# Attention stage of a graph transformer step: x and weights loaded in parts, projections by token halves, a column of ones beside the values, key and query sketches placed between projections

## What is computed

```
xn = layernorm(x)
q, k, v = xn @ Wq, xn @ Wk, xn @ Wv            # 8 heads of 64
phi(z)  = (0.125 * (z @ G1) * (z @ G2)) ** 2   # per head; G1, G2 are 64 x 64
kv      = phi(k).T @ v                          # per head 64 x 64
den     = phi(q) @ sum(phi(k), over tokens)
attn    = (phi(q) @ kv) / (den + 1e-6)
x       = x + biases + attn @ Wp
m       = relu(xn) + 1e-7                       # first message of the graph part
A[dst, src] += 1                                # adjacency of 20625 edges, sorted by dst
...                                             # 3 graph convolutions, then the experts
```

## Time and profile before

| what | value |
|---|---|
| median of 3 runs | 1040.75 us (1038.95 to 1041.92) |
| the profiled execution | 1040.16 us, of which the span of the core is 1038.3 us |
| mean granted TensorE clock in it | 0.954 |
| PE busy | 940.6 us (91%) |
| DVE busy | 709.4 us (68%) |
| ACT busy | 447.8 us (43%) |
| POOL busy | 392.2 us (38%) |
| first one-hot row of the adjacency | 156.7 us after the start |

### The profile page before, as it was taken

The page is one execution under the profiler, slowest core; times in us unless marked ns, Lnnn a source line. Parts: engine busy times, 40 slices in busy tenths (PEclk is TensorE's granted clock), DMA queues, the critical chain, the costliest instruction groups (busy, mean ns, idle before and its releaser), DMA issues. The chain is left out here.

```text
span 1038.3 us, 13178 instructions
## 1 busy us (share of the span) xinstructions
PE 940.6 (91%) x4324; PEld 696.8 (67%) x4324; DVE 709.4 (68%) x1325; ACT 447.8 (43%) x694; POOL 392.2 (38%) x322
## 2 busy tenths in 40 slices
PE   2979598996999999998999989889999999999980
PEld 2879585443888778886788868666666666666650
DVE  4463548988665467678767786758777776766675
ACT  3442510013344353543444522466666666666640
POOL 4500000000750035410751115366666666666640
PEclk9985898998999999999999998989999999999995
DMA  6200003312420022201220052559999999999868
GB/s 173 83 1 1 1 1 118 121 57 88 133 72 23 1 80 92 83 1 51 87 86 17 20 186 87 187 196 328 338 339 334 355 333 324 380 348 345 312 161 209
DMA packets 57100, 159.73 MB, mean 154 GB/s; under 512 B 13840, under 2 KB 21590, under 8 KB 48595
## 3 DMA queue, kind: packets, MB, share of 16 engines
q1 hardware_dynamic: 44755, 147.63, 41.7%
q0 software_dynamic: 12288, 11.36, 3.8%
HBM read 152.71 MB, written 25.58 MB: 172 GB/s over the span
## 5 line engine op out<-in xcount | busy, mean ns | idle before, releaser
L260 PE MATMUL ps<-split_operands 128*125 128x512 f32 (+5 forms) x690 | 272.9, 396 | 31.4 <-DVE split_operands L986 5.7
L261 PE MATMUL ps<-split_operands 128*125 128x512 f32 (+5 forms) x690 | 266.1, 386 | 0.0
L262 PE MATMUL ps<-split_operands 128*125 128x512 f32 (+5 forms) x690 | 265.4, 385 | 0.0
L630 POOL DMA_INDIRECT yrow_scratch<-work,row_i x64 | 150.9, 2358 | 97.3 <-ACT work L891 94.8
L260 PEld LDWEIGHTS ps<-split_operands 128*125 128x125 f32 (+3 forms) x690 | 135.0, 196 | 61.3 <-issue 13.6
L376 POOL TENSOR_TENSOR split_operands<-work,split_operands 128x512 fp32r<-128x512 f32 x66 | 83.6, 1296 | 202.1 <-ACT split_operands L358 189.9
L262 PEld LDWEIGHTS ps<-split_operands 128*125 128x125 f32 (+3 forms) x690 | 135.2, 196 | 26.7
L261 PEld LDWEIGHTS ps<-split_operands 128*125 128x125 f32 (+3 forms) x690 | 135.6, 196 | 24.0
L1366 DVE TENSOR_TENSOR gate_up_lo<-expert_weights,split_operands 128x2048 fp32r<-128x2048 f32 x64 | 146.3, 2286 | 3.8 <-ACT split_operands L873 3.6
L873 ACT ACTIVATE split_operands<-expert_weights 128x2048 fp32r<-128x2048 f32 x64 | 121.9, 1905 | 3.2 <-DMA expert_weights<-experts_in 3.1
L1834 PE MATMUL ps<-expert_weights,work 128*117 128x512 f32 x256 | 120.3, 592 | 0.5 <-issue 0.5
(11 more groups left out here) (214 smaller groups left out, 1286.3 us busy)
## 6 DMA issues: line engine op xcount, KB each, us to landing
expert_weights<-experts_in SPq DMA_DIRECT2D x64, 1024.0 KB
expert_weights<-experts_in SPq DMA_DIRECT2D x64, 512.0 KB
work<-w_in SPq DMA_DIRECT2D x12, 1024.0 KB, 5.2
yrow_scratch<-work SPq DMA_DIRECT2D x5, 1500.0 KB
split_operands<-yrow_scratch SPq DMA_DIRECT2D x4, 1120.0 KB
work<-wmix_in SPq DMA_DIRECT2D x4, 1024.0 KB, 7.6
work<-cw_in SPq DMA_DIRECT2D x3, 1024.0 KB, 5.2
work<-rows_in SPq DMA_DIRECT2D x10, 256.0 KB, 4.7
```

The costliest lines, as they stand in the source:

```text
L260: pe.matmul(o, a[1], b[0], start=start, stop=False)
L261: pe.matmul(o, a[0], b[1], start=False, stop=False)
L262: return pe.matmul(o, a[0], b[0], start=False, stop=stop)
L630: pool.indirect_dma_start(yrow, bass.IndirectOffsetOnAxis(ap=row_i[:, e:e + 1], axis=0), OS[e % 4], None, bounds_check=last_row, oob_is_er ...
```

## The change

- The plan holds Wv and Wk as two halves each. SP loads the first two tiles of x, the halves of Wv, then the other three tiles, the bias rows and the halves of Wk; ACT issues the last 13 rows of x. DVE does statistics and norms of two tiles first and of the others one at a time, between the work on the values. The transposes of tiles 2 to 4 stand inside the products of the values.
- The projections take a half of the tokens through all four chunks, then the other half.
- The low part of the values moves from POOL to DVE. The bias rows that POOL adds to x are summed first (6 additions in place of 10), and this is done after the query sketches.
- The value tiles are 130 columns a chunk, with a column of ones on either side (written by POOL). The key-value product is 15 instead of 25 matmuls a chunk, of 256 columns each that hold 128 values and the ones; the separate product with ones is gone. The evacuation of it takes 65 columns a head and chunk instead of 128.
- Key sketches start after six key projections and stand between the others; query sketches stand between the last query projections; the messages are done beside the first key projections.
- Membership is a comparison per tile boundary (4 operations instead of 10, 2 matmuls instead of 5), and the ranges are worked out in the third round of the attention output. The buffers of this preparation have places of their own, so that the index tables are made at the start.
- PE starts the adjacency without waiting for the last addition to x, and the zeros that clear the scratch in memory are ready from the start, so SP starts that clearing (5 transfers of 1500 KB) behind the attention weights instead of at the start of the adjacency.

```diff
-        VV = pair(o_e, NT, D, p=T)
-        KT = pair(o_e + 5120, KD, TP)
+        VV = pair(o_e, NT, KD * 130, p=T)
+        KT = pair(o_e + 5200, KD, TP)
...
-            return two_banks(4 if t % 2 else 6)
-
-        kv_bank = ps[:, 0:2, :].rearrange("p b (c n) -> p (b c) n", c=2)
+            b = 6 if t % 2 else 4
+            return ps[0:T, b:b + 2, :].rearrange("p b (c n) -> p (b c) n", c=2)
+
+        def values(v, t):
+
+            return v[:, t, :].rearrange("p (c n) -> p c n", c=KD)[:, :, 1:129]
+
+        def kv_window(c):
+
+            return cut(130 * c if c % 2 == 0 else 130 * (c + 1) - 256, 256)
+
+        def kv_out(c):
+
+            return ps[:, c // 2, cut(256 if c % 2 == 0 else 0, 256)]
+
+        def kv_part(h):
+
+            return ps[64 * h:64 * h + 64, 0:2, 126:386].rearrange("p b (a n) -> p b a n", a=2)[:, :, :, cut(65 * h, 65)]
...
-        piece("wv", wmv[2], WMA)
-        piece("wk", wmv[1], WMB)
+        for n, m, w in (("wv", 2, WMA), ("wk", 1, WMB)):
+            for k in range(2):
+                piece(f"{n}{k}", wmv[m][:, 2 * k:2 * k + 2, :], sub(w, A_, cut(2 * k, 2), A_))
...
-            by_rows(XO, x.rearrange("(t p) f -> p t f", p=T), "x_in", (sp, sp))
+            xv = x.rearrange("(t p) f -> p t f", p=T)
+            sp.dma_start(XO[0:112, 0:2, :], xv[0:112, 0:2, :]).then_inc(S("x_in"), 16)
...
-            for n in ("wv", "wk"):
-                load(n)
+            load("wv0")
+            load("wv1")
+            sp.dma_start(XO[0:112, 2:NT, :], xv[0:112, 2:NT, :]).then_inc(S("rw_in"), 16)
...
+            load("wk0")
+            load("wk1")
...
-            sp.wait_ge(S("vector_consts"), 2)
+            sp.wait_ge(S("vector_consts"), 1)
...
+            for t in range(NT):
+                for part in range(2):
+                    last = pool.memset(f(VV[part][:, t, :]).rearrange("p (c n) -> p c n", c=KD)[:, :, 0:130:129], 1.0 - part)
+            last.then_inc(S("pool_consts"), 1)
...
+            pool.wait_ge(S("pk_lo"), PKU + 8)
+            g1(pool.tensor_tensor(BC2, BC2, BC1[:, D:H], ALU.add))
             for t in range(NT):
-                g1(pool.tensor_tensor(XO[:, t, :], XO[:, t, :], BC1[:, D:H], ALU.add))
                 pool.tensor_tensor(XO[:, t, :], XO[:, t, :], BC2, ALU.add).then_inc(S("x_rows"), 1)
...
-                pool.wait_ge(S("v_hi"), t + 1)
-                pool.tensor_tensor(VV[1][:, t, :], MT[t % 2][0:T, :], f(VV[0][:, t, :]), ALU.subtract).then_inc(S("v_lo"), 1)
...
+            for u in range(3, 6):
+                proj(u)
+            act.wait_ge(S("v_lo"), NT)
+            pk_scale(0)
+            proj(6)
+            pk_square(0)
+            pk_scale(1)
+            proj(7)
+            pk_square(1)
+            proj_sb(8)
+            pk_scale(2)
+            pk_scale(3)
+            pk_square(2)
+            pk_scale(4)
+            pk_square(3)
+            proj_sb(9)
+            pk_square(4)
+            proj_hi(8)
+            proj_hi(9)
+            split_hi("wp")
+            proj(10)
+            proj(11)
...
+            proj(12)
+            proj(13)
             pq_scale(0)
-            for u in range(8):
-                if u + 1 < 8:
-                    pq_scale(u + 1)
-                pq_square(u)
+            proj(14)
+            pq_scale(1)
+            pq_square(0)
+            pq_scale(2)
+            pq_square(1)
+            proj(15)
+            for u in range(3, 8):
+                pq_scale(u)
+                pq_square(u - 1)
...
+            row_norm(0)
+            row_norm(1)
+            tr_lo(0)
+            split_lo("wv0", dve)
+            split_lo("wv1", dve)
+            tr_lo(1)
+            dve.wait_ge(S("rw_in"), 32)
+            row_var(2)
+            row_var(3)
+            row_norm(2)
+            dve.wait_ge(S("first_rows_in"), 64)
+            v_sum(0)
+            tr_lo(2)
+            row_norm(3)
+            row_var(4)
+            v_sum(1)
+            v_low(0)
+            tr_lo(3)
+            row_norm(4)
+            split_lo("wk0", dve)
...
+            for u in range(4):
+                message(0, u)
+                proj_lo(u)
+            message(0, 4)
+            proj_lo(4)
+            split_lo("wq", dve)
+            proj_lo(5)
+            pk_mul(0)
+            proj_lo(6)
+            pk_low(0)
+            pk_mul(1)
+            proj_lo(7)
...
+            proj_lo(12)
+            proj_lo(13)
+            pq_mul(0)
...
-            dve.memset(zero_b, 0.0).then_inc(S("vector_consts"), 1)
...
+                near = iota_odd[:, j // 2, :] if j % 2 else iota_h[:, cut(T * j, T + 1)]
...
-                        dve.tensor_scalar(one_hot_dst[:, i, :], iota_h[:, 0:T + 1], dstrel[:, j, bass.ds(lo + q * G + i, 1)], None,
+                        dve.tensor_scalar(one_hot_dst[:, i, :], near, dstf[:, bass.ds(lo + q * G + i, 1)], None,
...
-            for u in range(8, 16):
-                if u == 10:
-
-                    pe.wait_ge(S("pk_lo"), NT)
-                    pe.wait_ge(S("v_lo"), NT)
-                    pe.wait_ge(S("vector_consts"), 1)
-                    for c in range(KD):
-                        b, o = c // 2, 256 * (c % 2)
-                        for t in range(NT):
-                            mm3(ps[:, b, cut(o, P)], sub(PK, A_, t, cut(c * P, P)), sub(VV, A_, t, cut(c * P, P)), t == 0, t == NT - 1)
-                        for t in range(NT):
-                            for part in range(2):
-                                last = pe.matmul(ps[:, b, cut(o + P, P)], PK[part][:, t, cut(c * P, P)], ones_r[:],
-                                                 start=(t == 0 and part == 0), stop=(t == NT - 1 and part == 1))
...
+            def key_values():
+                pe.wait_ge(S("pk_lo"), NT)
+                pe.wait_ge(S("v_lo"), NT)
+                pe.wait_ge(S("pool_consts"), 3)
+                for c in range(KD):
+                    for t in range(NT):
+                        last = mm3(kv_out(c), sub(PK, A_, t, cut(c * P, P)), sub(VV, A_, t, kv_window(c)), t == 0, t == NT - 1)
+                last.then_inc(S("kv_ps"), 1)
+
+            def members():
+                pe.wait_ge(S("member"), 1)
+                for i in range(2):
+                    last = pe.matmul(ps[0:1, 6 + i, 0:2 * CH], ones_b[:, 0:1], member[:, cut(2 * CH * i, 2 * CH)], start=True, stop=True)
+                last.then_inc(S("member_ps"), 1)
...
+            for t in range(NT):
+                values_of(t)
+            weights("wk1")
+            pe.wait_ge(S("pool_consts"), 2)
+            for u in range(6):
+                proj(u)
+            weights("g")
+            pe.wait_ge(S("v_sb"), NT)
+            phi_k(0)
+            proj(6)
+            phi_k(1)
+            proj(7)
+            weights("wq")
+            proj(8)
+            phi_k(2)
+            phi_k(3)
+            phi_k(4)
+            proj(9)
+            proj(10)
+            proj(11)
+            key_values()
+            proj(12)
+            proj(13)
+            members()
+            phi_q(0)
+            proj(14)
+            phi_q(1)
+            phi_q(2)
+            proj(15)
+            for u in range(3, 7):
+                phi_q(u)
             attend(0)
-            for t in range(NT + 1):
+            phi_q(7)
+            attend(1)
+            attn_transpose(0)
+            weights("wp")
...
-            pe.wait_ge(S("mix_out_add"), NT)
-            pe.wait_ge(S("vector_consts"), 2)
+                mix_out(t - 1)
+```

How the instructions stand on three engines, in the kernel before and in the changed one:

The first transfers on SP (before; `wmix` holds Wv, then Wk, `rows` the biases):

```order
1 L256 DMA x_out<-x_in 112x5x512
2 L256 DMA x_out<-x_in 13x5x512
3 L402 DMA work<-wmix_in 128x4x512 x2
4 L406 DMA colp<-cols_in 128x63
5 L407 DMA work<-rows_in 128x512
```

432 lines of the change are left out of this document (224 added, 208 removed).

## The result

The changed kernel takes 997.95 us (median of 5 runs, 991.27 to 1000.15); the kernel before, in the same session, 1040.75 (1035.62 to 1043.64). The ratio is 0.9584, 95% interval 0.9551 to 0.9618: faster by 4%. The forecast was 998.

A forecast was written before the change was run, and what follows sets the result against it. PE was taken to bound the attention stage, though not full of useful work. Milestone terms summed to -45.3 us; allowances made it -42.6, and 1040.2 - 42.6 + 0.6 gave 998 us, range 989 to 1008 (chance 0.80).

The forecast's parts named there:

- To the values: Start of the attention stage: PE's first matmul of the values moves from 22.7 to 12.2 us.
- Values: First values product to first key projection: DVE sets the pace, 18.2 us, so keys start at 30.4 instead of 39.7.
- Keys and first queries: First key projection to key-value product: 28.8 us, 28.0 of it PE work; the product starts at 59.2 instead of 71.3.
- Key-value product: 60 matmuls of 256 columns at full clock: 7.1 us instead of 21; 12.8 if it stays at half clock.
- To the first product with Wp: End of key-value product to first Wp product: 25.1 us instead of 43.4, query sketches at a 1.9 us period.
- Output loop: Attention output products with Wp: 18.6 us instead of 18.3, with 1 us given to the ranges.
- Hand-over: PE's last attention matmul to DVE's first one-hot row: 1.4 us instead of 2.6.
- The allowance: Set against the sum of milestones: 2.0 us for one fall of the clock and 0.7 for hand-overs.
- The slower one: One-hot rows: comparisons slow down because their index table moves and is read at a shifted start, 1022 or 1064; chance 0.03.
- Half way: Attention stage: weights or x land late and sketches do not overlap, 1009 to 1035 us; chance 0.10.
- more: Attention stage: no clock fall, x at 4.1 and shorter ACT steps give 983 to 988 us; chance 0.06.

The follow-up runs named there:

- late_zeros: The changed kernel with POOL's memsets of key-value operands, ones and value columns put behind its last inverse root for x's norms: 994.78 us, ratio 0.9592.
- x_whole: The changed kernel with the rest of x sent ahead of Wv and DVE waiting for all of x: 1001.67 us, ratio 0.9644.
- queries_apart: The changed kernel with all query sketches in one piece behind the last two projections: 1000.30 us, ratio 0.9606.
- before_no_pause: The kernel before with its narrow key-value product unaltered but placed behind four query projections instead of two: 1026.76 us, ratio 0.9891.
- kv_130: The changed kernel with the key-value product in windows of 130 columns in place of 256, still 60 matmuls: 1000.08 us, ratio 0.9629.

## Why the prediction was right

The steps held, with one term off by 1.8 us, and an allowance of 2.7 that took it up. That forecast and median agree to 0.1 us is luck: the same kernel had a median of 999.41 in another session, and its two profiled executions took 991.27 and 999.19. Interval by interval, forecast and first trace:

- **To the values**, -10.5 forecast, -8.7 measured: the term that was off most. x landed at 5.03 (5.2 forecast), but the norms took 3.0 us instead of 1, held by POOL's memsets. The forecast took DVE's queue into account and not what POOL does beside it. late_zeros brings the start forward by 2.1 us, the first row by 1.45.
- **Values**, 18.2 forecast, 17.7 measured. Right in size for a wrong reason, which is luck: not DVE set the pace (15.0 of 17.8 us busy) but PE, full at 17.76, whose first matmuls run at half pace (below).
- **Keys and first queries**, 28.8 forecast, 29.0 measured; x_whole shows that PE has no air here. The cover was better than the sum had it: DVE was busy for 20.7 us and not 26, so the term did not hang on the 2.8 us of air that the forecast gave it.
- **Key-value product**, 7.1 forecast, 7.2 measured. That of the old 21.1 us nearly half was clock is shown by three runs. The product did not stay at half clock: nothing pauses in front of it, and 28.8 of the 28.9 us ahead of it PE is busy.
- **To the first product with Wp**, 25.1 forecast, 24.9 measured. The spacing of 1.9 us is there (82.20 to 84.10 between two multiplications), with `attend(0)` and `attend(1)` in the gaps. This is the largest term, and the least tested. How the 18.5 us won here divide among the moved projections, DVE's tables, the shorter chain and the clock (low for 16.9 us of this part before, by the 0.83, 0.83 and 0.68 of the earlier trace rows, and never in the first trace after) was not tried part by part; queries_apart says that the three early sketches have about 1 of them, and before_no_pause that DVE's work ahead of the sketches could cost PE 7.
- **Output loop**, 18.6 forecast, 18.2 measured: the ranges cost nothing. **Hand-over**, 1.4 forecast, 1.9 measured: 1.2 us of it is DVE's own, between its last addition and its first row.
- **The allowance** of 2.0 us for one fall of the clock and 0.7 for hand-overs. The first trace had no fall, the second had one, worth about 0.4 at the first row. What filled the allowance was the first item.
- **The rivals.** The slower one is refuted by both comparisons of a row. The first reads the moved table: 378 ns as before. The second is the one that reads it at a shifted start; before, then after:

```profile
L1119 DVE TENSOR_SCALAR work<-work x175: 242/250/260, 157.0 to 246.1; 125x126 bf16<-125x126 f16 x175
```

```profile
L1225 DVE TENSOR_SCALAR work<-work x175: 241/249/257, 113.3 to 201.4; 125x126 bf16<-125x126 f16 x175
```

"Half way" and "more" did not occur.

## What to carry to other kernels

A pause of PE can cost twice: its own length, and the clock behind it for as long as it then stays down. Here the clock that fell behind 2.4 us of waiting cost 10 us more, since it stayed down through all of the 100 narrow matmuls that came next; the pause of 2.73 us in the first trace of the changed kernel had no fall behind it; moving work that is ready into the pause was worth nearly as much (11.3 us at the first row) as rewriting the product (13.2). And when a start-up chain is short, look at what an engine does beside it that shares no data with it: memsets that nobody waits for held the one operation that everybody waited for.

## What was not expected of the hardware

- Matmuls of 128 or 130 columns of these operands take 0.112 us at full clock and 0.21 at half, nearly what 256 columns take (0.120 and 0.213).
- The first matmuls of the values run at half pace, 0.43 us for 512 columns where 0.23 follows, for 8 matmuls in the first trace and 6 to 14 in others, while the window's granted clock reads 1.00. The clock's record in each trace begins just where that pace ends (17.6 us in the first), so the clock may well have stood at its lower level until then: 512 columns in 0.427 us are 1.2 a ns. The values take 17.7 us in the first trace and 18.9 in that of kv_130, 1.2 more.
- POOL's memsets, two of 128 x 1024 values (0.94 us each) and small ones behind them, from 7.58 to 9.92, beside DVE's `tensor_scalar` made two of these take 3.01 us instead of 1.00.
- The clearing of 7.5 MB beside the one-hot rows, at a DMA share of 0.34, cost them 0.7 us of 88, and not by slower comparisons: loads of one number into a register took 0.98 us (PE) and up to 1.21 (DVE) at the second tile, where they take 0.31 without it.
